# Recurrent two-axis block kernel: z staged in SBUF, weights folded one call ahead, exclusive sums read as shifted inclusive ones

## What is computed

```
zxbcdt = rmsnorm(x) @ Win;  z = zxbcdt[..., :128]
xBC = silu(causal_conv(zxbcdt[..., 128:288]))      # x heads 8x16, B and C of 16 states
dt = softplus(zxbcdt[..., -8:] + dt_bias);  A = -exp(A_log)
cum = cumsum(dt * A);  decay = exp(cum_l - cum_s) where s <= l
scores = (C_l . B_s) * decay * dt_s;  y = scores @ xh     # forward, plus the same reversed
y = y + D * xh
y = rmsnorm(y * silu(z)) * gn_w;  x = x + y @ Wout
```

## Time and profile before

| | us |
|---|---|
| median of 3 runs (lowest, highest) | 2950.7 (2944.52, 2956.05) |
| the profiled execution: its own time | 2953.49 |
| its span, first to last instruction | 2951.5 |
| busy: PE, DVE, ACT, POOL | 2153.9, 1981.8, 1744.2, 1079.7 |
| share of the span: PE, DVE, ACT, POOL | 73%, 67%, 59%, 37% |
| first squares of call 0; last `y_ready` copy (L1305) | 904.9; 2928.9 |

### The profile page before, as it was taken

One profiled execution on the slowest core, in us unless ns is written; L12 is line 12 of the kernel. 1 busy time (PEld: TensorE's weight loads), 2 busy tenths in 40 slices (PEclk: granted clock), 3 DMA queues, 4 the chain that ended last, 5 costly groups with the idle time before them and its releaser, 6 DMA issues. The chain is left out here.

```text
span 2951.5 us, 64266 instructions
## 1 busy us (share of the span) xinstructions
PE 2153.9 (73%) x26182; PEld 1100.1 (37%) x26182; DVE 1981.8 (67%) x2779; ACT 1744.2 (59%) x2811; POOL 1079.7 (37%) x827
## 2 busy tenths in 40 slices
PE   4277777776774887698688588658857886885886
PEld 3022222222221553354255245325524542552553
DVE  2587888888877566565666656565765666666564
ACT  1266766766653575477367457536754773674574
POOL 0044444444451343244045235304522531451342
PEclk6588888888896998799799799869978988997998
DMA  4000000000001111110111111011111101111111
GB/s 133 0 0 1 0 1 0 1 0 0 1 0 29 32 34 28 35 33 15 44 38 26 38 27 40 15 31 32 34 36 26 42 15 39 33 25 30 32 34 31
DMA packets 96695, 74.59 MB, mean 25 GB/s; under 512 B 69392, under 2 KB 77584, under 8 KB 95120
## 3 DMA queue, kind: packets, MB, share of 16 engines
q1 hardware_dynamic: 96400, 70.48, 10.0%
HBM read 20.62 MB, written 8.39 MB: 10 GB/s over the span
## 5 line engine op out<-in xcount | busy, mean ns | idle before, releaser
L892 POOL TENSOR_TENSOR SQ<-SQ 128x512 f32<-128x512 f32 x344 | 467.2, 1360 | 708.4 <-ACT SQ L811 425.1
L859 POOL TENSOR_TENSOR Y<-Z 128x512 f32<-128x512 f32 x256 | 330.8, 1292 | 531.6 <-DVE Z L1096 297.7
L807 ACT ACTIVATE O<-bank 128x512 f32<-128x512 f32 x512 | 304.3, 594 | 210.2 <-PE bank L571 207.5
L1293 DVE TENSOR_TENSOR SQ<-bank,O 128x512 f32<-128x512 f32 x344 | 236.2, 689 | 163.8 <-issue 118.8
L571 PE MATMUL bank<-SS,work 32*128 32x512 bf16 x512 | 203.7, 398 | 169.3 <-ACT O L807 168.2
L892 POOL TENSOR_TENSOR SQ<-O,SQ 128x512 f32<-128x512 f32 x168 | 226.9, 1350 | 254.8 <-PE bank L592 185.7
L1096 DVE TENSOR_TENSOR_SCAN Z<-bank,SS 128x512 f32<-128x512 f32 x256 | 311.0, 1215 | 0.5
L536 PE MATMUL bank<-folded_weights,work 128*64 128x128 f32 x4096 | 300.1, 292 | 0.0
L463 PE MATMUL bank<-Y,constants 128*128 128x512 f32 x512 | 295.5, 662 | 6.2 <-DVE bank L1104 4.6
L592 PE MATMUL bank<-folded_weights,work 128*32 128x64 f32 x8192 | 287.3, 230 | 11.3 <-POOL SQ L892 10.8
L512 PE MATMUL bank<-XP,block_weights 128*128 128x512 f32 x256 | 156.9, 725 | 174.3 <-DVE Z L1227 174.3
(11 more groups left out here) (271 smaller groups left out, 3990.2 us busy)
## 6 DMA issues: line engine op xcount, KB each, us to landing
work<-XP SPq DMA_DIRECT2D x256, 134.0 KB
work<-extra SPq DMA_DIRECT2D x768, 8.0 KB
decay_cols_kept<-extra SPq DMA_DIRECT2D x48, 128.0 KB, 1.8
SS<-decay_cols_kept SPq DMA_DIRECT2D x384, 16.0 KB
block_weights<-callw SPq DMA_DIRECT2D x8, 735.0 KB, 4.4
Z<-state_sel SPq DMA_DIRECT2D x1, 2048.0 KB, 13.2
out<-O SPq DMA_DIRECT2D x2, 1024.0 KB, 8.5
constants<-consts SPq DMA_DIRECT2D x1, 1347.5 KB, 6.1
```

Source lines behind the costliest of these rows:

```text
L807: A(D2C[u % 2], bank[2], ACT.Copy).then_inc(sg("d2_copied"), 1)
L859: g.tensor_tensor(hc[t_ % 4], hs[t_ % 4], c_copy[t_ % 4], ALU.mult).then_inc(sg("s1_hc"), 1)
L892: g.tensor_tensor(MM[u % 2].rearrange("p (h l) -> p h l", l=L), DK[u % 3].rearrange("p (h l) -> p h l", l=L), GM[(u // 8) % 2][:, 64 * (u ...
L1293: v.tensor_tensor(DK[u % 3], bank[u % 2], D2C[u % 2], ALU.min).then_inc(sg("decay_least"), 1)
```

## The change

- **z.** All sixteen z matmuls move into the front, through five banks (4, 5, 7, 0, 1). ACT copies each from PSUM to Z2 (`copy_z`). Inside the steps, at tau = 4i - 2, ACT takes tanh of Z2's block into tz and DVE gates it in place (`gate_z`), both now out of SBUF. The first `project_bc`, `project_x`, their tanh and their gates move ahead of the step loop.
- **Weights.** There are two sets, FW2. `fold(c, piece)` has eight pieces; the set of call c + 1 is made at tau = 32 to 39 of call c, one piece a step, ahead of that step's L1293. The set of call 0 is made once ahead of the calls, after stage 1.
- **Sums.** dE and its split are gone. Q is formed from dL and dF read one element earlier within each sequence. Only F is stored to DRAM. The E columns are F's columns read back one element later: a DMA of 2 x 64 runs of 63 elements of 2 bytes, beside a plain one, three of each a group.
- **Issue.** The six row DMAs of Q for group 0 are issued from ACT's queue instead of SP's.

```diff
-        FW = sb("folded_weights", 1856)
+        FW2 = [sb(f"folded_weights{i}", 1856) for i in range(2)]
...
+        tz = O[:, 3584:4096]
+        z_banks = [4, 5, 7, 0, 1]
...
+        def z_due(tau):
+
+            i, r = divmod(tau + 2, 4)
+            return i if r == 0 and 0 <= i < 16 else None
...
+                        sp.wait_ge(sg("split_P"), c + 1)
+                    decay_rows(sp, g, 0, "P")
+                    if g > 0:
+                        sp.wait_ge(sg("split_Q"), c + 1)
+                        decay_rows(sp, g, 1, "Q")
+                    if g == 0:
+                        sp.wait_ge(sg("decay_stored"), (c + 1) * 48)
+                    for j in range(3):
+                        kept = cols_dram[j, 16 * g:16 * g + 16, :]
+                        sp.dma_start(RHS[g % 2][2 * j:2 * j + 2, :], kept.rearrange("(b h) n -> b (h n)", h=8)).then_inc(
+                            sg(f"decay_cols{g % 2}"), 16)
+                        sp.dma_start(RHS[g % 2][32 + 2 * j:34 + 2 * j, :].rearrange("b (n l) -> b n l", l=L)[:, :, 1:L],
+                                     kept.rearrange("(b h) (u l) -> b (h u) l", h=8, l=L)[:, :, 0:L - 1]).then_inc(
+                            sg(f"decay_cols{g % 2}"), 16)
...
+                sp.wait_ge(sg("split_F"), c + 1)
+                for j in range(3):
+                    sp.dma_start(cols_dram[j], SPLIT["F"][j]).then_inc(sg("decay_stored"), 16)
...
+                    if i >= 5:
+                        pe.wait_ge(sg("z_copied"), c * 16 + (i - 4))
+                    mm(bank[z_banks[i % 5]], W(f"wz{i % 2}"), xn_group(i // 2), start=True, stop=True).then_inc(
+                        sg("z_psum"), 1)
...
+                project_bc(0)
+                project_x(0, 0)
+                project_x(0, 1)
+                for i in range(5, 16):
+                    z(i)
+                pe.wait_ge(sg("z_copied"), c * 16 + 16)
+                pe.wait_ge(sg("dt_added"), c + 1)
...
+                def copy_z(i):
+                    act.wait_ge(sg("z_psum"), c * 16 + i + 1)
+                    A(Z2[:, z_at(i)], bank[z_banks[i % 5]], ACT.Copy).then_inc(sg("z_copied"), 1)
+
+                for i in range(5):
+                    copy_z(i)
                 act.wait_ge(sg("dt_bounded"), c + 1)
                 A(dL, dL, ACT.Ln).then_inc(sg("dL_ready"), 1)
...
                 act.wait_ge(sg("folded"), c + 1)
+                hbbc = folded(c)[7]
+                tanh_bc(0)
+                tanh_x(0)
+                for i in range(5, 16):
+                    copy_z(i)
+                act.wait_ge(sg("split_Q"), c + 1)
+                decay_rows(act, 0, 1, "Q")
...
+                    i = z_due(tau)
+                    if i is not None:
+                        act.wait_ge(sg("z_copied"), c * 16 + i + 1)
+                        if i >= 1:
+                            act.wait_ge(sg("z_ready"), c * 16 + i)
+                        A(tz, Z2[:, z_at(i)], ACT.Tanh, scale=0.5).then_inc(sg("z_tanh"), 1)
...
+            def fold(c, piece):
...
+                if piece == 0:
+                    dve.wait_ge(sg(f"block_weights_loaded{c % 2}"), c // 2 * 16 + 16)
+                    for t, name in enumerate(("cxa", "cxb")):
+                        v.tensor_tensor(wx[t], W("wx"), W(name), ALU.mult)
...
+            for piece in range(8):
+                fold(0, piece)
...
-                v.tensor_tensor(dE, dF, dA_, ALU.subtract).then_inc(sg("dE_ready"), 1)
-                dve.wait_ge(sg("dE_ready"), c + 1)
                 dve.wait_ge(sg("dL_ready"), c + 1)
                 order(v.tensor_tensor(dP, dL, dF, ALU.subtract))
-                dve.wait_ge(sg("cast_E"), 2 * c + 1)
-                v.tensor_tensor(rest_e, dE, SPLIT["E"][0], ALU.subtract).then_inc(sg("rest_E"), 1)
...
+                v.tensor_copy(grid(dQ)[:, :, 0:1], grid(dL)[:, :, 0:1])
+                order(v.tensor_tensor(grid(dQ)[:, :, 1:L], grid(dL)[:, :, 1:L], grid(dF)[:, :, 0:L - 1], ALU.add))
+                for name, src, ready in (("P", dP, "split_P"), ("Q", dQ, "split_Q")):
+                    hi, mid, lo = SPLIT[name]
+                    order(v.tensor_copy(hi, src))
+                    order(v.tensor_tensor(rest_v, src, hi, ALU.subtract))
+                    order(v.tensor_copy(mid, rest_v))
+                    v.tensor_tensor(lo, rest_v, mid, ALU.subtract).then_inc(sg(ready), 1)
+                    dve.wait_ge(sg(ready), c + 1)
...
+                def gate_z(i):
+                    dve.wait_ge(sg("z_tanh"), c * 16 + (i + 1))
+                    v.scalar_tensor_tensor(Z2[:, z_at(i)], tz, 1.0, Z2[:, z_at(i)], ALU.add, ALU.mult).then_inc(
+                        sg("z_ready"), 1)
...
+                gate_b(0)
+                gate_c(0)
+                gate_x(0)
+                dve.wait_ge(sg("split_F"), c + 1)
                 for tau in range(FIRST, LAST):
+                    if 32 <= tau < 40 and c + 1 < 8:
+                        fold(c + 1, tau - 32)
...
-                    for i in Z_SLOTS.get(tau, ()):
+                    i = z_due(tau)
+                    if i is not None:
```

More of the change, by code:

```diff
@@ L625, in call @@
                         g = every(tau, 8, offset, NGROUP)
-                        if g is not None:
+                        if g is not None and (g > 0 or offset != -8):
                             work_(g)
@@ L1297, in call @@
                         k = every(tau, 4, offset, 16)
-                        if k is not None:
+                        if k is not None and (k > 0 or offset != -3):
                             work_(k)
@@ L1301, in call @@
                         g = every(tau, 8, offset, NGROUP)
-                        if g is not None:
+                        if g is not None and (g > 0 or offset > -5):
                             work_(g)
```

211 lines of the change are left out of this document (78 added, 133 removed).

## The result

| | before | changed |
|---|---|---|
| median (range), us | 2947.8 (2944.5 to 2956.1) | 2981.8 (2977.3 to 2985.3) |
| span of the profiled execution, us | 2951.5 | 2975.3 |
| mean granted TensorE clock | 0.857 | 0.839 |

The changed kernel takes 1.011 times the time of the one before, 95% interval 1.0086 to 1.0133: 1.1% slower, against a forecast of 3.5% faster.

The account below looks back on a forecast made before the run. PE was taken to bound the kernel: its own order in the front, its pace in the steps. Terms -12.2 - 14 + 10 + 2.5 = -13.7 a call, -109.6 for eight, plus 4.9 once, gave 2848 us, range 2780 to 2932.

Parts of the forecast that it names:

- A: Front of each call: first decay matmul earlier, -12.2 us a call (from -2 to -14).
- Rival 4: Shifted column reads land late, stalling steps and front: +27 us a call, 3173 us; chance 0.04.
- the second rival's low clock: Front: z matmuls run at the low clock, 10.3 us a call, 2931 us; chance 0.09.
- its first form: Front: DMAs issued on ACT and SP take turns, 3.8 us a call, 2879 us; no separate chance given.
- B: First two groups of each call, freed of z matmuls: -14 us a call (from -10.3 to -19).
- C: Tanh and gate of z inside every group of steps: +10 us a call (from 0 to 29).
- D: Weights folded in one group of steps: +2.5 us a call (from 0 to 5).
- E: Weight set of call 0 made once, ahead of the third group norm's sum over X: +4.9 us.
- the third: DVE and ACT become the steps' pace, at tau mod 8 = 2: 3.0 us a group, 3010 us; chance 0.06.
- rival 1: Work added in the steps is hidden, so more is gained: -25.7 us a call, 2755 us; chance 0.14.
- settled groups past 23.2 us: Steps: settled groups, forecast at 22.3 us, passing 23.2 us would show the prediction wrong.

Follow-up runs that it names:

- Run 12: Run 10 with the three shifted column reads replaced by plain ones (decay sums then not exclusive): 2740.5 us, ratio 0.930 to the kernel before.
- run 1: Changed kernel without tanh and gate of z in the steps, z left ungated: 2817.6 us, ratio 0.957 to the kernel before.
- run 15: Run 10 plus heavy idle matmuls in its step-6 waits and six in the front's wait: 2723.5 us, ratio 0.924 to the kernel before.
- run 13: Changed kernel with three heavy idle f32 matmuls in the wait of step 6 of each eight: 2927.1 us, ratio 0.992 to the kernel before.
- 16: Kernel before, with only heavy idle matmuls (512 and 256 columns) added in its step-6 waits: 2932.4 us, ratio 0.995.
- run 4: Changed kernel, tanh kept, gate replaced by a same-size operation with one operand in PSUM: 2834.8 us, ratio 0.961 to the kernel before.
- run 5: Changed kernel with tanh and gate of each group's odd half moved from step 2 to step 7: 2833.4 us, ratio 0.961 to the kernel before.
- run 6: Run 5 with the fold pieces also moved, one in each eighth step behind its other work: 2790.7 us, ratio 0.946 to the kernel before.
- 8: Changed kernel with Silu on ScalarE replacing the copies, tanh and gate of z: 2821.4 us, ratio 0.957 to the kernel before.
- run 10: Changed kernel with Silu replacing tanh and gate of z, and fold pieces one in each eighth step: 2765.5 us, ratio 0.938 to the kernel before.

## Why the prediction was wrong, point by point

**A, front: right but for the landing.** -9.0 a call for -12.2. Counted from the call's first squares, SP's stores of F were to start at 29.8 us, the rows of P to end at 36.0 and the columns' issue at 39.2; they did at 30.0, 35.8 and 39.6. I gave shifted reads the 1.8 us of the earlier trace rows behind the end of their issue; that is a plain store's time, and from the start of its issue. The first decay matmul came 4.7 us behind the end of the last one's issue (4.5 to 5.2 in the eight calls). Run 12, with plain reads, shortens a front by 2.7 us, most of the difference. Rival 4 saw these reads as the risk, but in the steps and by throughput; in the steps no L581 waits for a DMA, and in the front it was latency. The z matmuls ran at full clock (twelve records in 5.42 us), so the second rival's low clock is out. Neither can its first form hold, DMAs on ACT and SP taking turns: the six on SP's queue and the six on ACT's overlapped and took 4.5 and 4.4 us to issue.

**B, first groups: about right, and the close sum is luck.** -12.2 a call with C's share against -12.4. Without tanh and gate (run 1) it is -15.9 for my -14, so C's share was 3.6 us a call for my 1.6, and the two misses cancel. I had allowed 5 us for the low clock; run 15 without it takes 33.1 for my 38.

**C, tanh and gate: the step that failed.** The place and order were as I walked through them; the sizes weren't. Without both (run 1) steps 17 to 64 are 140 us shorter than in the changed kernel and the first 16 are 29 shorter: 21 us a call for my 10. That lies inside C's own range of 0 to 29; the range of the whole, up to 2932, didn't leave room for it. Three terms are in it:
- The gate. I had the rule and the rows for it and priced it near L1276's 0.891, for the whole of which the product must miss it. In this order it meets one nearly each time: 1.35.
- What stands behind it. I took the gate's own length as its delay. It also moves `add_squares` onto a product (0.89 to 1.80). Such a price belongs to a position, not to a line, and the position changes with everything ahead of it.
- The clock, which I had only in the front and the first groups. The 48 steps behind the table loads take 293.5 us in the changed kernel and 218.2 before; with their waits filled (13 and 16) they take 194.8 in both. So at this place alone 75 of the 190 us, 9.4 a call, are clock. Another 49 us, 6.2 a call, are the longer wait ahead of it, and 42 are in step 4, where the later scores, the fold pieces and the clock meet. (Steps 17 to 64 of 13 and 16 still differ by 155 us, since the clock of run 13 fell at step 4 instead.)

The Trainium skill, page "SBUF — State Buffer", section "Who interferes with whom", has the later of the two instructions block until the first is done. The trace agrees in the main: the instructions end 0.54 us behind the product that they met, a little less than the 0.68 that one takes alone, and run 4's, which reads PSUM, never take more than 0.690.

**D, fold pieces: too low, and hidden.** 1.4 us in each of the seven calls that have them in the changed kernel, for my 2.5 (which the sum took eight times); 6 to 8 (runs 5 and 6, 8 and 10) once the gate is out of the way, over my upper bound of 5. I had taken half of the work as the price. What it costs that a piece stands ahead of L1317 in eight steps in a row I left out; one piece in each eighth step, behind its other work, takes that away (run 6).

**E:** +6.0 for +4.9. In two runs with the same work there (6 and 13) it is +2.8 and +2.6, so only its rough size is confirmed.

**The rival that held** is the third, to which I gave 0.06: the place (step 2 of each eight), 3.0 us a group and 3010 us. Measured are 23.5 and 24.7 us (2.6 and 3.8 over 20.9) in the two groups of call 1 ahead of the fold pieces, 24.9 in the mean over all calls where 21.5 stood, and 2982. But its mechanism, DVE and ACT as the pace, isn't what happened: DVE is busy for 17.8 of 24.7 us, and the same load, placed elsewhere, leaves 20.9 (run 6). It is one chain, gate to `add_squares` to table loads to copy, and TensorE's clock behind it. My sign "settled groups past 23.2 us" came true. (The rival's arithmetic is sound; that of rival 1, -25.7 a call, gives 2750, not 2755.)

## What to carry to other kernels

A VectorE instruction with two SBUF operands beside a busy GpSimd is to be priced at its worst meeting (here 1.7 to 1.8 us, not 0.69), and so is every such instruction behind it; then ask which wait hangs on that place in the order, since the same work three steps earlier cost little (tanh and gate together 16 us, run 5 against run 1). When a wait of TensorE grows, the matmuls behind it may take twice as long, so count them in; and a cost that an experiment finds small may only be lying behind a larger one. When a filled wait keeps its clock, look where the clock falls next.

## What the runs showed of the hardware

- TensorE behind its step-6 wait. Where the two matmuls around it start 3 us or more apart, the step behind was at the lower clock in all 39 cases of the changed kernel; where 2.7 to 2.9 us, in all 6 of the changed kernel, but in 14 of 48 before and 15 of 48 in run 10. Filling the wait with twelve 32-row bf16 matmuls (2.76 us busy) left 45 of 48 over 5 us; filling it with three 128-row f32 ones (2.84 us busy) left none of 48, though more steps then ran low elsewhere (25 of 40 behind step 4, for 11). A busy PE in the profile isn't yet one that keeps its clock. Idle matmuls that feed nothing took 55 us off the changed kernel and 42 off version 10.
- Reads from DRAM in 126-byte runs, shifted by one element: the matmul that waits for them starts 4.5 to 5.2 us after the last issue ends (eight calls). The plain stores of 128 KB next to them land 1.4 us after the end of their issue, 1.8 after its start. With plain reads instead (run 12) a front is 2.7 us shorter.
- A VectorE instruction with two SBUF operands (128x512 f32) that starts while GpSimd's product runs ends 0.54 to 0.55 us behind that product's end, in 80 gates and 40 `add_squares` of the changed kernel; one that meets none takes 0.68 to 0.69.
- Silu from PSUM takes what a copy takes (0.60 us for 128x512 in the median, both), but the runs with Silu have four more table loads of 1.283 us a call, two for Silu and one each for the logarithm and the exp behind it.
